# Weight copies in quarters instead of halves, and a second exponential buffer in the prefix pass

## The chip, the cores and the metric

One Trainium2 chip, all 8 cores, each running the same program on its own data with no exchange between them. Core c works on sequence c // 2 and on half c % 2 of its 4096 positions. The time is the device time of the slowest core in microseconds.

## The reference

A block with a state space part and a quantised feed-forward part, both fed with the same normalised input, on x of shape (4, 4096, 1024):

```python
xn = _layernorm(x, axis=-1)
x = x + _L0_attn_ref(xn, ...) + _L0_ffn_ref(xn, w_gate, w_up, w_down)

# _L0_attn_ref, D_MODEL 1024, D_INNER 2048, D_STATE 16:
x = _rmsnorm(resid, norm_w)
skip = x @ skip_w.T
x = x @ in_w.T
x = silu(_causal_depthwise_conv(x, conv_w, conv_b))
A = -jnp.exp(A_log)
delta = softplus(x @ wd1.T @ wd2.T + wd2_b)
Bm = x @ wb.T
Cm = x @ wc.T
# scan over positions: h = exp(dt*A) * h + (dt*x) * B ; y = sum_n h * C
y = _selective_scan(x, delta, Bm, Cm, A)
y = (y + x * W_D) * silu(skip)
return resid + y @ out_w.T
```

## The kernel before

A core owns 2048 positions (T) of a sequence. The state with which the scan of its half starts depends on the first half of the sequence, so every core also works through that prefix (`x_pre`), and a mask makes the result zero where the core owns the first half. D is 1024, E (the inner width) 2048 and thus 16 tiles of 128 channels (`ET`), the states are 16 (`NS`), taken 8 at a time (`nh`), and positions go in chunks of 512 (`CH`, 4 of them).

The stages in order of time: quantising and transposing of the feed-forward weights with the normalisation of the own half; the feed-forward part; the normalisation of the prefix; `p3_chunks` for the prefix; then `p3_prefix` and `p3_chunks` for the own half, interleaved by `drive`; `p3_scan` for the own half; the output projection.

`p3_chunks` first copies its weights into SBUF as bf16. `inwT` (1024 x 2048 float32) is taken as 8 blocks of 128 rows and each block in two halves: SyncE loads a half (128 x 1024 float32, 512 KB) into `tmpc`, and VectorE casts it into `inw_sb`. There is one `tmpc`, and SyncE waits for the last cast before the next load. For the own half `skipwT` follows in the same way, into `skw_sb`. Then come the four chunks; the first matmul of the first chunk waits for all of VectorE's work so far.

`p3_prefix` computes the state at the end of the prefix without a scan for each state: for each tile of 128 channels it loads delta (`dtile`) and x (`xct`), forms `dxt` (their product) and `cbuf` (the running sum of delta), and 8 biases. Then, for each of 8 states, ScalarE computes E = exp(scale * cbuf + bias) into `Eb[j]`, VectorE the product `ub` = dxt * B, and then the sum over positions of E * ub, in place in `Eb[j]` with its sum in `acc1`, which is copied to a column of `h0_sb`. `Eb` is `[xct, xct]`, so both entries are the tile that held x, and `E_free` is the count of VectorE's work after which ScalarE may write E again. Four small matmuls a step, whose results nobody uses, follow VectorE's instructions on TensorE.

`drive` gives one tile of `p3_prefix` and one chunk of `p3_chunks` alternately: tile 0, then the weight copies and chunk 0, tile 1, chunk 1, and so on; after chunk 3 the other 28 of 32 tiles stand alone. Each engine takes its instructions in the order written. Two helpers issue most of them: VectorE's all have line 54 and each waits for the one before it; ScalarE's have line 103; loads have line 130 and wait for the load before them on the same semaphore.

Of the kernel before, what the change touches and what calls it, by code (L numbers as in the profile page):

```python
# [14 lines left out]
D, E, NS, DTR, I, T = 1024, 2048, 16, 64, 2816, 2048  # L15
# [160 lines left out]
def build_nc(upto="full", dbg=None):  # L176
    nc = bass.Bass("TRN2", target_bir_lowering=False)
    kb = KB(nc)
# [6 lines left out]
    inwT = dr("inwT", [D, E])  # L185
    skipwT = dr("skipwT", [D, E])
# [343 lines left out]
    with contextlib.ExitStack() as st:  # L530
        sb = lambda n, s, dt=F32: st.enter_context(nc.sbuf_tensor(n, s, dt))
# [160 lines left out]
    def p3_chunks(xrT_src, own, sdel, sxcd, sBd, sCd, psums=None):  # L692
      def _gen():
        with contextlib.ExitStack() as st:
            sb = lambda n, s, dt=F32: st.enter_context(nc.sbuf_tensor(n, s, dt))
            pre = "c3o" if own else "c3p"
            inw_sb = sb(pre + "_inw", [128, 8, E], BF16)
            tmpc = sb(pre + "_tmpc", [128, E // 2])
            _xi0 = sb(pre + "_xi0", [128, 3 + CH])
            xib = [_xi0, _xi0]  # L700
            cb = sb(pre + "_cb", [128, CH])
# [7 lines left out]
            if own:  # L709
                skw_sb = sb(pre + "_skw", [128, 8, E], BF16)  # L710
# [8 lines left out]
            else:  # L719
                ps_x, ps_dl, ps_B, ps_C, ps_d2, ps_sk = psums  # L720

            for dt_ in range(8):
                for hh in range(2):
                    @B.sync
                    def _(sync):
                        kb.wait(sync, "V")
                        kb.wait(sync, "S")
                        kb.wait(sync, "St")
                        kb.wait(sync, "Tn")
                        kb.dma(sync, tmpc[:], inwT.rearrange("(a p) e -> p a e", p=128)[:, dt_, hh * (E // 2):(hh + 1) * (E // 2)])  # L730
                    ldv = kb.cnt["L"]

                    @B.vector
                    def _(vector):
                        vector = kb.wrap(vector, "V")
                        kb.wait(vector, "L", ldv)
                        kb.inc(vector.tensor_copy(inw_sb[:, dt_, hh * (E // 2):(hh + 1) * (E // 2)], tmpc[:]), "V")
            if own:
                for dt_ in range(8):
                    for hh in range(2):  # L740
                        @B.sync
                        def _(sync):
                            kb.wait(sync, "V")
                            kb.dma(sync, tmpc[:], skipwT.rearrange("(a p) e -> p a e", p=128)[:, dt_, hh * (E // 2):(hh + 1) * (E // 2)])
                        ldv = kb.cnt["L"]

                        @B.vector
                        def _(vector):
                            vector = kb.wrap(vector, "V")
                            kb.wait(vector, "L", ldv)  # L750
                            kb.inc(vector.tensor_copy(skw_sb[:, dt_, hh * (E // 2):(hh + 1) * (E // 2)], tmpc[:]), "V")

            for c in range(NCH):
                sba = SBatch(kb)
# [137 lines left out]
                sba.flush(B)  # L892
                yield
      return _gen()

    if upto == "p1pre":
# [197 lines left out]
    def p3_prefix():  # L1094
        with contextlib.ExitStack() as st:
            sb = lambda n, s, dt=F32: st.enter_context(nc.sbuf_tensor(n, s, dt))
            Brep = sb("pf_Brep", [128, 8, T], BF16)
            dtile = sb("pf_dt", [128, T])
            xct = sb("pf_xct", [128, T])
            dxt = sb("pf_dxt", [128, T])  # L1100
            Eb = [xct, xct]
            ub = sb("pf_ub", [128, T])
            cbuf = sb("pf_c", [128, T])
            onescol = sb("pf_ones", [128, 1])
            bias2 = sb("pf_bias", [128, NS])
# [5 lines left out]
            @B.vector  # L1111
            def _(vector):
                vector = kb.wrap(vector, "V")
                vector.memset(onescol[:], 1.0)
                vector.tensor_scalar(nA_sb[:], A_sb[:], -1.0, None, ALU.mult)

            E_free = [kb.cnt["V"], kb.cnt["V"]]

            for nh in range(2):
                @B.sync  # L1120
                def _(sync):
                    kb.wait(sync, "V")
                    kb.wait(sync, "S")
                    if nh == 0:
                        kb.wait(sync, "St")
                    kb.dma(sync, Brep[:], sB[nh * 8:nh * 8 + 8, :].partition_broadcast(128))
                ldb = kb.cnt["L"]

                for et in range(ET):
                    @B.sync  # L1130
                    def _(sync):
                        kb.wait(sync, "V")
                        kb.wait(sync, "S")
                        kb.dma(sync, dtile[:], sdelta[et * 128:(et + 1) * 128, :])
                        kb.dma(sync, xct[:], sxc[et * 128:(et + 1) * 128, :])
                    ldt = kb.cnt["L"]

                    @B.vector
                    def _(vector):
                        vector = kb.wrap(vector, "V")  # L1140
                        kb.wait(vector, "L", max(ldt, ldb))
                        vector.tensor_tensor(dxt[:], dtile[:], xct[:], ALU.mult)
                        vector.tensor_tensor_scan(cbuf[:], ones, dtile[:],
                                                  zero1[:], ALU.mult, ALU.add)
                    v_dx = kb.cnt["V"]

                    sba = SBatch(kb)
                    s_E = [0] * 8
                    v_bias = [0] * 8
                    for n in range(8):  # L1150
                        col = et * NS + nh * 8 + n

                        @B.vector
                        def _(vector):
                            vector = kb.wrap(vector, "V")
                            vector.tensor_tensor(bias2[:, n:n + 1], A_sb[:, col:col + 1],
                                                 cbuf[:, T - 1:T], ALU.mult)
                        v_bias[n] = kb.cnt["V"]

                    for n in range(8):  # L1160
                        j = n % 2
                        col = et * NS + nh * 8 + n
                        sba.wait("V", v_bias[n])
                        if E_free[j]:
                            sba.wait("V", E_free[j])
                        s_E[n] = sba.act(Eb[j][:], cbuf[:], AF.Exp,
                                         scale=nA_sb[:, col:col + 1],
                                         bias=bias2[:, n:n + 1])

                        @B.vector  # L1170
                        def _(vector):
                            vector = kb.wrap(vector, "V")
                            vector.tensor_tensor(ub[:], dxt[:], Brep[:, n, :], ALU.mult)
                            kb.wait(vector, "S", s_E[n])
                            vector.scalar_tensor_tensor(Eb[j][:], Eb[j][:], 1.0, ub[:],
                                                        ALU.mult, ALU.mult, accum_out=acc1[:])
                            E_free[0] = E_free[1] = kb.cnt["V"]
                            vector.tensor_copy(h0_sb[:, col:col + 1], acc1[:])
                        v_pf = kb.cnt["V"]

                        @B.tensor
                        def _(tensor):
                            for pc in (v_pf - 2, v_pf - 1, v_pf):
                                kb.wait(tensor, "V", pc)
                                tensor.matmul(ps_hp[:], eye_sb[:], eye_sb[:, 0:128],  # L1185
                                              start=True, stop=True)
                            kb.inc(tensor.matmul(ps_hp[:], eye_sb[:], eye_sb[:, 0:128],
                                                 start=True, stop=True), "Tn")
                    sba.flush(B)
                    yield  # L1190
# [23 lines left out]
    with contextlib.ExitStack() as st:  # L1214
        sb = lambda n, s, dt=F32: st.enter_context(nc.sbuf_tensor(n, s, dt))
        oww = sb("c4_oww", [128, ET, D], BF16)
        tmpc = sb("c4_tmp", [128, D])
# [130 lines left out]
```

How the kernel before makes its waits and increments, by code:

```python
        def wrapped(*a, **k):  # L51
            if kb.cnt[sem] > 0:
                eng.wait_ge(kb.sems[sem], kb.cnt[sem])
            instr = attr(*a, **k)
            instr.then_inc(kb.sems[sem], 1)
            kb.cnt[sem] += 1
            return instr
# [28 lines left out]
        @B.scalar  # L86
        def _(scalar):
            for it in items:
                if it[0] == "wait":
                    _, sem, v = it
                    scalar.wait_ge(kb.sems[sem], v)
                else:
                    _, my, out, in_, func, scale, bias, accum_out = it
                    if my > 1:
                        scalar.wait_ge(kb.sems["S"], my - 1)
                    kw = {}
                    if scale is not None:
                        kw["scale"] = scale
                    if bias is not None:
                        kw["bias"] = bias
                    if accum_out is not None:
                        kw["accum_out"] = accum_out
                    scalar.activation(out=out, in_=in_, func=func, **kw).then_inc(kb.sems["S"], 1)
# [23 lines left out]
    def dma(self, eng, out, in_, sem="L"):  # L127
        if self.cnt[sem] > 0:
            eng.wait_ge(self.sems[sem], self.cnt[sem])
        return self.inc(eng.dma_start(out=out, in_=in_), sem, 16)
# [1 line left out]
    def wait(self, eng, sem, val=None):  # L132
        v = self.cnt[sem] if val is None else val
        if v > 0:
            eng.wait_ge(self.sems[sem], v)
```

## Time and profile before

| | us |
|---|---|
| median of 2 runs | 11219.18 |
| lowest and highest | 11208.52, 11229.85 |
| profiled execution, its device time | 11207.93 |
| its span, slowest core | 11206.4 |
| spans of the eight cores | 11175.8 to 11206.4 |

The profile is that of the slowest core. The span is the time from its first instruction to its last, 1.5 us less than the execution's device time. The eight cores lie within 0.3% of each other, with a mean granted TensorE clock of 0.641 to 0.645 of full speed. The stage with `p3_prefix` in it runs from about 4998 to 8259 us.

### The profile page before, as it was taken

The numbers are of one execution on the slowest core, as the hardware profiler recorded it, in microseconds if no ns is written. First come the engines' busy times: TensorE is split into PE (matmuls) and PEld (weight loads), VectorE is DVE, ScalarE is ACT, GpSimd is POOL, SyncE is SP. The second block draws the span as 40 slices with busy tenths as digits, with TensorE's granted clock in tenths as the row PEclk, the third lists the DMA queues.
The fourth block names the chain that finished last, engine by engine and source line by source line (L and its number), as shares of the span: only waits on it lengthen the run. The fifth ranks groups of instructions, "written<-read, shape, count | busy, mean of one in ns | idle before, by whom it ended". The sixth has DMA issues, their size and how long they took to land.

```text
span 11206.4 us, 49419 instructions; the slowest of 8 cores (11175.8 to 11206.4 us)
## 1 busy us (share of the span) xinstructions
PE 2902.3 (26%) x8880; PEld 961.5 (9%) x8880; DVE 5942.8 (53%) x6033; ACT 2255.6 (20%) x2926; POOL 0.2 (0%) x4
## 2 busy tenths in 40 slices
PE   0101111454454123322344321111112222222224
PEld 0000000111111000000011100000000000000001
DVE  4444444344344122222323347777779997999950
ACT  1111111111111312210211222323322222222200
POOL 0000000000000000000000000000000000000000
PEclk9999999776676555555556555555555555555557
DMA  1111111100101011112111111010011112111112
GB/s 35 34 37 30 34 38 43 41 12 18 53 29 36 27 47 38 38 53 72 43 50 32 42 47 38 30 53 33 35 71 45 43 37 80 53 67 52 68 60 72
DMA packets 222951, 493.65 MB, mean 44 GB/s; under 512 B 115328, under 2 KB 115968, under 8 KB 198272
## 3 DMA queue, kind: packets, MB, share of 16 engines
q1 hardware_dynamic: 222656, 490.49, 13.0%
q8 instruction: 90, 1.47, 0.1%
q14 instruction: 205, 1.68, 0.1%
HBM read 330.27 MB, written 160.17 MB: 44 GB/s over the span
## 4 chain that ended last, share of the span: by engine, by line
DVE 52%; DMA 15%; PE 14%; ACT 9%; issue 9%; DVEq 1%; ACTq 1%; SPq 0%
DVE s3o_hb L54 10%; DVE pf_xct L54 5%; DVE pf_ub L54 5%; DVE s3o_ub L54 5%; DVE s3o_hcb L54 3%; PE c3o_pssk L834 2%; PE c3p_psx L768 2%; DVE c3o_cb L54 2%; DVE c3p_cb L54 2%; DVE q_t L54 2%; ACT L103 2%; DMA pf_dt<-sdelta 1%; DMA pf_xct<-sxc 1%; ACT q_wide L103 1%; PE c3o_psx L768 1%
## 5 line engine op out<-in xcount | busy, mean ns | idle before, releaser
L54 DVE TENSOR_TENSOR_SCAN s3o_hb<-s3o_ab,h_sb,s3o_ub 128x2048 bf16<-128x2048 f32 x256 | 1147.7, 4483 | 83.9 <-ACT s3o_ab L103 58.5
L103 ACT ACTIVATE s3o_ab<-s3o_dt,A_sb 128x2048 f32<-128x2048 f32 x256 | 513.1, 2004 | 1427.5 <-DVE s3o_hb L54 1412.8
L103 ACT ACT_TABLE_LOAD x196 | 251.5, 1283 | 2477.3 <-PE q_ps L389 845.9
L1031 PE MATMUL s3o_psht<-eye_sb 128*128 128x128 bf16 x768 | 203.3, 265 | 1859.8 <-DVE s3o_hb L54 1164.1
L103 ACT ACTIVATE pf_xct<-pf_c,pf_bias,pf_nA 128x2048 f32<-128x2048 f32 x256 | 536.8, 2097 | 676.2 <-DVE pf_xct L54 655.7
L1185 PE MATMUL pf_psht<-eye_sb 128*128 128x128 bf16 x768 | 201.5, 265 | 1756.3 <-DVE pf_ub L54 1207.0
L54 DVE TENSOR_TENSOR pf_ub<-pf_dxt,pf_Brep 128x2048 f32<-128x2048 f32 x256 | 586.9, 2293 | 27.3 <-DVE h_sb L54 0.8
L54 DVE SCALAR_TENSOR_TENSOR pf_xct<-pf_xct,pf_ub 128x2048 f32<-128x2048 f32 x256 | 586.8, 2292 | 27.4 <-DVE pf_ub L54 0.9
L54 DVE TENSOR_TENSOR s3o_ub<-s3o_dxt,s3o_Brep 128x2048 f32<-128x2048 f32 x256 | 586.8, 2292 | 27.0 <-DVE s3o_dxt L54 0.5
L1038 PE MATMUL s3o_psy<-s3o_hcb,eye_sb 128*128 128x512 bf16 x1024 | 477.4, 620 | 3.0 <-issue 0.6
L389 PE MATMUL q_ps<-eye_sb,q_wq 128*128 128x128 bf16 x528 | 140.2, 266 | 1212.7 <-DVE q_wq L54 868.1
L54 DVE TENSOR_TENSOR p_h<-p_h,p_psu 128x512 f32<-128x512 f32 (+1 forms) x96 | 61.8, 643 | 739.3 <-ACT p_h L103 739.3
L54 DVE TENSOR_REDUCE q_bm<-q_w 128x64 f32<-128x1024 f32 (+1 forms) x52 | 78.4, 1507 | 561.3 <-DMA q_w<-wu 202.0
L54 DVE TENSOR_TENSOR s3o_hcb<-s3o_hb,s3o_Crep 128x2048 bf16<-128x2048 bf16 x256 | 313.7, 1225 | 27.5 <-DVE s3o_hb L54 0.9
L103 ACT ACTIVATE p_hqT<-p_pst 128x128 bf16<-128x128 bf16 x352 | 97.9, 278 | 979.9 <-PE p_pst L623 979.9
L54 DVE COPY c3o_xi<-halo_sb 128x3 f32<-128x3 f32 x64 | 10.8, 169 | 532.3 <-ACT c3o_xi L103 532.3
L583 PE MATMUL p_psg<-p_wgh,xqT_sb 128*128 128x512 bf16 (+1 forms) x768 | 236.5, 469 | 170.5 <-DMA p_wdh<-swdT 75.3
L54 DVE TENSOR_TENSOR pf_dxt<-pf_dt,pf_xct 128x2048 f32<-128x2048 f32 x32 | 73.4, 2292 | 377.6 <-DMA pf_xct<-sxc 377.6
L1031 PEld LDWEIGHTS s3o_psht<-eye_sb 128*128 128x128 bf16 x768 | 79.8, 104 | 2166.1 <-issue 2166.1
L623 PE MATMUL p_pst<-eye_sb,p_hq 128*128 128x128 bf16 x352 | 87.9, 250 | 605.6 <-DVE p_hq L54 457.0
L1185 PEld LDWEIGHTS pf_psht<-eye_sb 128*128 128x128 bf16 x768 | 79.9, 104 | 1898.2 <-issue 1898.2
L638 PE MATMUL p_psd<-p_wdh,p_hqT 128*128 128x512 bf16 x352 | 217.2, 617 | 55.1 <-ACT p_hqT L103 55.1
(161 smaller groups left out, 5846.0 us busy)
## 6 DMA issues: line engine op xcount, KB each, us to landing
pf_dt<-sdelta SPq DMA_DIRECT2D x32, 1024.0 KB, 4.8
pf_xct<-sxc SPq DMA_DIRECT2D x32, 1024.0 KB, 4.8
s3o_dt<-sdelta_o SPq DMA_DIRECT2D x32, 1024.0 KB, 6.5
s3o_xct<-sxc_o SPq DMA_DIRECT2D x32, 1024.0 KB, 4.8
sxc<-c3p_xc SPq DMA_DIRECT2D x64, 256.0 KB, 2.3
sdelta<-c3p_db SPq DMA_DIRECT2D x64, 256.0 KB, 2.3
sxc_o<-c3o_xc SPq DMA_DIRECT2D x64, 256.0 KB, 2.3
sskip<-c3o_skb SPq DMA_DIRECT2D x64, 256.0 KB, 2.3
```

Source lines behind the costliest of these rows:

```text
L54: instr = attr(*a, **k)
L103: scalar.activation(out=out, in_=in_, func=func, **kw).then_inc(kb.sems["S"], 1)
L389: kb.inc(tensor.transpose(qps[pj][:], wqbf[j][:, jt * 128:(jt + 1) * 128], eye_sb[:]), "Tn")
L583: tensor.matmul(ps_g[jsi][:, :sl], xqT_sb[:, kd, tt * 128:(tt + 1) * 128], wgh[:, kd, s0:s0 + sl], start=(kd == 0), stop=(kd == 7))
L623: kb.inc(tensor.transpose(ps_t[pj][:], hq[jsp][:, isub * 128:(isub + 1) * 128], eye_sb[:]), "Tn")
L638: tensor.matmul(ps_d0[:], hqT[jsp][:, isub, :], wdh[:, it, 0:512], start=first, stop=last)
L768: mi = tensor.matmul(ps_x[jx][:], inw_sb[:, kd, et * 128:(et + 1) * 128], xrT_src[:, kd, c0:c0 + CH], start=(kd == 0), stop=(kd == 7))
L834: mi = tensor.matmul(ps_sk[:], skw_sb[:, kd, et * 128:(et + 1) * 128], xrT_src[:, kd, c0:c0 + CH], start=(kd == 0), stop=(kd == 7))
L1031: tensor.matmul(ps_ht[:], eye_sb[:], eye_sb[:, 0:128], start=True, stop=True)
L1038: mi = tensor.matmul(ps_y[sg][:], eye_sb[:], hcb[j][:, sg * 512:(sg + 1) * 512], start=(n == 0), stop=(n == 7))
L1185: tensor.matmul(ps_hp[:], eye_sb[:], eye_sb[:, 0:128], start=True, stop=True)
```

## The change

Three edits. The staging tile `tmpc` becomes half as wide (E // 4 columns), and the weight copies of `p3_chunks`, for the prefix and for the own half, take each block of 128 rows in four quarters instead of two halves. In `p3_prefix`, `Eb` gets a second buffer `_E1`, so that its two entries are different tiles, and `E_free` is kept for each of them. The tile for `ub` is dropped, and `ub` becomes another name of `dtile`.

```diff
-            tmpc = sb(pre + "_tmpc", [128, E // 2])
+            tmpc = sb(pre + "_tmpc", [128, E // 4])
...
+            EQ = E // 4
             for dt_ in range(8):
-                for hh in range(2):
+                for hh in range(4):
                     @B.sync
                     def _(sync):
                         kb.wait(sync, "V")
                         kb.wait(sync, "S")
                         kb.wait(sync, "St")
                         kb.wait(sync, "Tn")
-                        kb.dma(sync, tmpc[:], inwT.rearrange("(a p) e -> p a e", p=128)[:, dt_, hh * (E // 2):(hh + 1) * (E // 2)])
+                        kb.dma(sync, tmpc[:], inwT.rearrange("(a p) e -> p a e", p=128)[:, dt_, hh * EQ:(hh + 1) * EQ])
...
-                        kb.inc(vector.tensor_copy(inw_sb[:, dt_, hh * (E // 2):(hh + 1) * (E // 2)], tmpc[:]), "V")
+                        kb.inc(vector.tensor_copy(inw_sb[:, dt_, hh * EQ:(hh + 1) * EQ], tmpc[:]), "V")
             if own:
                 for dt_ in range(8):
-                    for hh in range(2):
+                    for hh in range(4):
                         @B.sync
                         def _(sync):
                             kb.wait(sync, "V")
-                            kb.dma(sync, tmpc[:], skipwT.rearrange("(a p) e -> p a e", p=128)[:, dt_, hh * (E // 2):(hh + 1) * (E // 2)])
+                            kb.dma(sync, tmpc[:], skipwT.rearrange("(a p) e -> p a e", p=128)[:, dt_, hh * EQ:(hh + 1) * EQ])
...
-                            kb.inc(vector.tensor_copy(skw_sb[:, dt_, hh * (E // 2):(hh + 1) * (E // 2)], tmpc[:]), "V")
+                            kb.inc(vector.tensor_copy(skw_sb[:, dt_, hh * EQ:(hh + 1) * EQ], tmpc[:]), "V")
...
-            Eb = [xct, xct]
-            ub = sb("pf_ub", [128, T])
+            _E1 = sb("pf_E1", [128, T])
+            Eb = [xct, _E1]
+            ub = dtile
...
-                            E_free[0] = E_free[1] = kb.cnt["V"]
+                            E_free[j] = kb.cnt["V"]
```

## Rows read from the trace of the kernel before

**Rows 1.** The page, part 1: busy us of each engine, share of the span, instructions.

```profile
PE 2902.3 (26%) x8880; PEld 961.5 (9%) x8880; DVE 5942.8 (53%) x6033; ACT 2255.6 (20%) x2926; POOL 0.2 (0%) x4
```

**Rows 2.** Busy time by stretch: the three weight copies (length, then each engine).

```profile
core 5: us, PE busy (x) PEld busy (x) DVE busy (x) ACT busy (x) POOL busy (x), PEclk, DMA share, GB/s
3950.60:4025.40 74.80, 0.00 (x1) 0.03 (x2) 11.11 (x16) 0.00 (x0) 0.00 (x0) 0.50 0.35 112
5074.50:5152.40 77.90, 0.01 (x1) 0.00 (x0) 11.11 (x16) 0.00 (x0) 0.00 (x0) 0.50 0.35 108
5152.40:5224.60 72.20, 0.00 (x0) 0.00 (x1) 11.11 (x16) 0.00 (x0) 0.00 (x0) 0.50 0.37 116
```

**Rows 3.** Timeline, start of the `skipwT` copy: start us, us, what, idle before.

```profile
5152.38 13.57 SPq L130 DMA_DIRECT2D c3o_tmpc<-skipwT  x4
5155.95 0.69 DVE L54 CAST c3o_skw<-c3o_tmpc 128x1024 bf16<-128x1024 f32 x1 [3.70 <-DMA c3o_tmpc<-skipwT]
5160.24 0.69 DVE L54 CAST c3o_skw<-c3o_tmpc 128x1024 bf16<-128x1024 f32 x1 [3.60 <-DMA c3o_tmpc<-skipwT]
```

**Rows 4.** Waits of the first matmuls for the last cast: own half, then prefix.

```profile
PE c3o_psx L768 <- DVE c3o_skw L54: 150.1, 1, 150.1
...
DVE c3p_inw L54: 75.5, 1
```

**Rows 5.** Timeline of the prefix loop, first two steps of a tile.

```profile
7619.92 1.28 ACT L103 ACT_TABLE_LOAD   x1 [20.52 <-DVE pf_bias L54]
...
7621.21 2.10 ACT L103 ACTIVATE pf_xct<-pf_c,pf_bias,pf_nA 128x2048 f32<-128x2048 f32 x1
7621.68 2.29 DVE L54 TENSOR_TENSOR pf_ub<-pf_dxt,pf_Brep 128x2048 f32<-128x2048 f32 x1
7624.08 2.29 DVE L54 SCALAR_TENSOR_TENSOR pf_xct<-pf_xct,pf_ub 128x2048 f32<-128x2048 f32 x1
...
7626.48 0.15 DVE L54 COPY h_sb<-pf_acc 128x1 f32<-128x1 f32 x1
...
7626.53 2.10 ACT L103 ACTIVATE pf_xct<-pf_c,pf_bias,pf_nA 128x2048 f32<-128x2048 f32 x1 [3.22 <-DVE pf_xct L54]
7626.74 2.29 DVE L54 TENSOR_TENSOR pf_ub<-pf_dxt,pf_Brep 128x2048 f32<-128x2048 f32 x1
...
7629.14 2.29 DVE L54 SCALAR_TENSOR_TENSOR pf_xct<-pf_xct,pf_ub 128x2048 f32<-128x2048 f32 x1
```

**Rows 6.** Groups of instructions, 4990 to 8260 us: the prefix loop's, with `dxt`.

```profile
L54 DVE TENSOR_TENSOR pf_ub<-pf_dxt,pf_Brep 128x2048 f32<-128x2048 f32 x256 | 586.9, 2293 | 27.3 <-DVE h_sb L54 0.8
L54 DVE SCALAR_TENSOR_TENSOR pf_xct<-pf_xct,pf_ub 128x2048 f32<-128x2048 f32 x256 | 586.8, 2292 | 27.4 <-DVE pf_ub L54 0.9
L103 ACT ACTIVATE pf_xct<-pf_c,pf_bias,pf_nA 128x2048 f32<-128x2048 f32 x256 | 536.8, 2097 | 676.2 <-DVE pf_xct L54 655.7 <-DVE h_sb L54 20.1
...
L54 DVE TENSOR_TENSOR pf_dxt<-pf_dt,pf_xct 128x2048 f32<-128x2048 f32 x32 | 73.4, 2292 | 377.6 <-DMA pf_xct<-sxc 377.6
```

**Rows 7.** Groups of VectorE with shapes apart: a cast of 128x512.

```profile
L54 DVE CAST c3o_xcbf<-c3o_xc 128x512 bf16<-128x512 f32 x64 | 27.3, 427 | 71.2 <-ACT c3o_xc L103 71.2
```

**Rows 8.** The staging tile of the own half: duration ns, starts, landing.

```profile
L130 SPq DMA_DIRECT2D c3o_tmpc<-inwT x16: 327/328/333, 5074.6 to 5147.6; - x16
L54 DVE CAST c3o_inw<-c3o_tmpc x16: 693/694/695, 5078.2 to 5151.6; 128x1024 bf16<-128x1024 f32 x16
...
DMA to landing us min/median/max: 3.3/3.5/4.4
```

**Rows 9.** DMA issues of the whole program: KB each, median us to landing.

```profile
pf_xct<-sxc SPq DMA_DIRECT2D x32, 1024.0 KB, 4.8
...
sxc<-c3p_xc SPq DMA_DIRECT2D x64, 256.0 KB, 2.3
...
c3p_tmpc<-inwT SPq DMA_DIRECT2D x16, 512.0 KB, 3.5
...
c3o_tmpc<-skipwT SPq DMA_DIRECT2D x16, 512.0 KB, 3.5
...
p_tmp<-wbT_c SPq DMA_DIRECT2D x1, 128.0 KB, 2.0
```

## Prediction

> **What bounds the kernel now.** I read the page's busy part first [rows 1]: VectorE is busy 53% of the span, ScalarE 20%, TensorE 26%. No engine fills the span, so what an edit is worth has to be read from its own stage. The diff touches two stages: the copying of weights at the start of `p3_chunks` (three times: `inwT` for the prefix, `inwT` and `skipwT` for the own half), and the inner loop of `p3_prefix`.
>
> The table by stage [rows 2] cuts out the three weight copies: 74.80, 77.90 and 72.20 us, together 224.9 us, in each of which VectorE is busy for 11.11 us (16 casts) and TensorE and ScalarE for nothing. That is a chain with no overlap: SyncE waits for the last cast, issues a load, VectorE waits for it, casts. The instructions in order of time [rows 3] show one round: the load is issued at 5152.38, the cast starts at 5155.95 (3.57 us later), lasts 0.69 us, and the next cast starts 4.29 us after this one. While this runs TensorE waits for the last cast: 150.1 us in the own half and 75.5 in the prefix [rows 4]. So the copies lie on the path in full.
>
> The prefix loop is the other case. In order of time [rows 5] its step is TENSOR_TENSOR (`ub`) 2.29 us, SCALAR_TENSOR_TENSOR with its sum 2.29, a column copy 0.15, and again: 5.06 us from one SCALAR_TENSOR_TENSOR to the next (7624.08 to 7629.14). The exponential of ScalarE, 2.10 us, starts at 7626.53, just after the sum is done with the one E buffer, runs beside the next `ub` product and ends at 7628.63. VectorE is done with `ub` at 7629.03 and starts the sum at 7629.14. So the exponential is ready 0.51 us before it is used. The groups of instructions say the same for all 256 steps [rows 6]: VectorE is idle for 27.4 us before the sums, 0.107 us each, and the same 27.3 before the `ub` products, which wait for nobody; its releaser is `pf_ub` on VectorE itself, not ScalarE. ScalarE does wait, 655.7 us in total, for the E buffer, but it is not the engine that is late.
>
> **The change, part by part.**
>
> *A second E buffer (`Eb = [xct, _E1]`, `E_free[j]`).* It takes away a wait of ScalarE: exponential n may start when sum n-2 is done instead of sum n-1. The chain through ScalarE is, per step, 0.16 us from the end of the sum to the exponential, 2.10 of exponential, about 0.11 to the sum and 2.29 of sum: 4.66 us, against VectorE's own chain of 5.06 [rows 5]. The longer one sets the pace and stays as it is: gain 0. From above the gain is bounded by all the idle time of VectorE before the sums, 27.4 us [rows 6]. At the first step of a tile the exponential starts late, since an activation table is loaded (1.28 us) after the biases are there; even there it ends at 7623.31 and is used at 7624.08, 0.77 us later [rows 5]. In the steady state exponential n starts at the end of sum n-2 and so again lies beside a `ub` product, one step ahead; only the second exponential of each tile moves to stand beside the first product and sum. VectorE's instructions should not lengthen by that: a product lasts 2293 ns with an exponential beside it (`ub`) and 2292 with ScalarE idle (`dxt`) [rows 6]. I cost this at 0.
>
> *`ub = dtile`.* The product goes into the tile that held delta. Both readers of delta, the `dxt` product and the scan, stand ahead of the first `ub` product on VectorE's own queue, and the next load of `dtile` already waits for everything of VectorE and ScalarE, before and after. No instruction and no wait is added: 0.
>
> *The weight copies in quarters.* 48 loads of 512 KB with 48 casts of 1024 columns become 96 loads of 256 KB with 96 casts of 512 columns; each round keeps its waits. Every wait, issue and landing is paid twice as often. The mean round is now 224.9 / 48 = 4.69 us. Of it two terms shrink. The cast: 128x1024 float32 to bf16 takes 694 ns [rows 8]; the very shape it becomes, 128x512, takes 427 [rows 7], so 0.27 less. The landing: 3.5 us for 512 KB [rows 8, 9]. A load of 256 KB is not in the trace. From below, 128 KB took 2.0; stores of 256 KB, to DRAM with the same 2 KB rows, took 2.3. From above, the step from 1024 KB (4.8) to 512 KB (3.5) is 1.3 us, and half of that off again gives 2.85; and at worst it doesn't shrink, 3.5 [rows 9]. Between the loads of 128 KB (2.0) and 512 KB (3.5) a straight line gives 2.5, and this is the value I take: it lies between the store and the extrapolation. So a round shrinks by 1.0 + 0.27 = 1.27 us:
>
> 2 x 224.9 - 96 x 1.27 = 449.8 - 121.9 = 327.9 us, which is 103 more than 224.9.
>
> The same with the ends: landing 2.0 gives +55, 2.3 gives +84, 2.85 gives +137, 3.5 gives +199. Nothing hides any of it, as TensorE, ScalarE and the rest of VectorE's queue stand behind the last cast.
>
> The Trainium skill (DMA: Bandwidth & Descriptors, Anatomy of one DMA) fits a transfer to 2.0 us fixed and bytes over 436 GB/s, measured on the other issuing path; the estimate from it is 3.2 for 512 KB and 2.6 for 256 KB, a drop of 0.60 where I take 1.0, and the sum would be +142. The trace's 3.5 for 512 KB lies 0.3 above that fit. The page also advises loads of 1 MiB and more, so it speaks against halving them.
>
> The first queue entries behind these waits are the chunk's first matmuls; they start later by the sum, and with them all that follows. The prefix's tiles 1 to 3 stand behind the chunks on every engine and move too. Sum: 11207.9 (the profiled execution, span 11206.4) + 0 + 0 + 103 = 11311. The median of the runs is 11219.2, 11.3 higher; on it the sum is 11322. I forecast 11315, between the two.
>
> **The rivals.**
>
> *The small loads are hidden or cost nothing (no change, 11208 to 11219).* This needs a second load in flight. Against it: the copy into the quarter tile waits as the one into the half tile did, there is still one `tmpc`, and TensorE waited 150.1 us for the last cast [rows 4].
>
> *The second E buffer was what was missing (faster).* If the sum on VectorE waited for ScalarE, double buffering would pay. For: ScalarE's 655.7 us of waiting, which looks like lost time. Against: the idle time before the sum is no longer than before the product [rows 6]. To be over 2% faster, 224 us, on top of the 103 of the copies, it must save 327 / 256 = 1.28 us a step; the time would be 10,984 to 10,995. It decides only where the exponential is longer than 2.10 + 0.51 us or VectorE's chain under 4.66.
>
> *A small load takes as long as a large one or longer (slower by over 2%).* Place: the same 96 rounds. If no term shrinks, +224.9, which is 11433 to 11444, 2.0% over. This decides from a landing of 3.77 us (then 0.27 of the cast is made up). For: rows of 2 KB are the shorter ones, and the eight cores load at once; single landings reach 4.4 us now [rows 8]. Against: each class of smaller load landed sooner [rows 9].
>
> *VectorE is slowed by ScalarE running ahead.* Were the sums a tenth longer, 256 x 0.23 = 59 us more: 11370 to 11381. It decides from any lengthening at all, since VectorE has no slack. No row shows a sum beside an exponential; against it stand the products, 2293 and 2292 ns, with and without one [rows 6].
>
> **How the numbers follow.** The forecast's case, the copies on the path with a landing between 2.0 and 3.5 and the prefix loop unmoved, has 0.88 and 11263 (11207.9 + 55) to 11418 (11219.2 + 199). Hidden loads 0.03, faster through the E buffer 0.02, no shrinking at all 0.04, slowed VectorE 0.03. I cut the upper end a little, since a landing of over 3.3 us contradicts three classes of rows: the range is 11260 to 11400, and the case of the slowed VectorE lies in it. Within 2%, about what a measurement of this kernel can tell from no change: 0.94. Slower by over 2% 0.04, faster 0.02.
>
> **What would show it.** In the profile after: 32 loads of 256 KB in each of the three copies, landing near 2.5 us; casts of 427 ns; the three copies 110, 113 and 105 us long, give or take 15; TensorE's wait for `skw` near 218 us instead of 150. In the prefix loop still 5.06 us per step, VectorE idle about 27 us before the sums, and ScalarE's wait for them down to about 192 x 2.96 = 570 us (two exponentials of each of 32 tiles now start without it). A step shorter than 5.06 would refute my reading of the loop; landings of 3.5 would refute the size of the copies' cost.

## The result

| | us |
|---|---|
| before, median of 6 runs | 11225.01 |
| after, median of 7 runs (11334.58 to 11347.67) | 11342.9 |
| ratio, 95% interval | 1.0109 (1.0097 to 1.0122) |
| profiled execution after, span of its slowest core | 11339.0 |

The change costs 1.1%, some 118 us between the medians and 132.6 us between the spans of the two profiled executions (11206.4 and 11339.0). The slowest core is core 7 now and was core 5. The page's first part after the change:

```profile
PE 2904.6 (26%) x8880; PEld 964.3 (9%) x8880; DVE 5951.1 (52%) x6081; ACT 2252.2 (20%) x2926; POOL 0.2 (0%) x4
```

Against [rows 1] no engine has more than 8.3 us of work added: VectorE has 48 more instructions (the casts) and 8.3 us more. So over 120 us came as waiting. The busy time by stretch, the three weight copies after the change (length, then each engine, as in [rows 2]), tells where:

```profile
3951.80:4071.20 119.40, 0.00 (x0) 0.00 (x0) 13.62 (x32) 0.00 (x0) 0.00 (x0) 0.50 0.23 70
5127.60:5245.70 118.10, 0.00 (x0) 0.00 (x0) 13.67 (x32) 0.00 (x0) 0.00 (x0) 0.50 0.23 71
5245.70:5360.80 115.10, 0.00 (x0) 0.00 (x0) 13.66 (x32) 0.00 (x0) 0.00 (x0) 0.50 0.25 73
```

They last 352.6 us together where they lasted 224.9: 127.7 of the 132.6 us. The staging tile of the own half, the first matmul's wait, and the loads' landing (the time from the issue of a load until its data is there), which answer to [rows 4, 8, 9]:

```profile
L54 DVE CAST c3o_inw<-c3o_tmpc x32: 426/427/428, 5130.5 to 5245.1; 128x512 bf16<-128x512 f32 x32
...
  PE c3o_psx L769: 233.4, 1
...
DMA to landing us min/median/max: 2.7/2.8/3.6
```

A cast takes 427 ns instead of 694, a load lands after 2.8 us instead of 3.5, and there are twice as many of both; TensorE waits 233.4 us for the last cast instead of 150.1.

The prefix loop, groups of instructions from 4990 to 8400 us, answers to [rows 6] (`ub` is shown as `pf_dt` now, since it shares delta's tile):

```profile
L54 DVE TENSOR_TENSOR pf_dt<-pf_dxt,pf_Brep 128x2048 f32<-128x2048 f32 x256 | 586.9, 2293 | 27.8 <-DVE h_sb L54 1.5
L54 DVE SCALAR_TENSOR_TENSOR pf_xct<-pf_xct,pf_dt 128x2048 f32<-128x2048 f32 x128 | 293.4, 2292 | 13.7 <-DVE pf_dt L54 0.5
L54 DVE SCALAR_TENSOR_TENSOR pf_E<-pf_E,pf_dt 128x2048 f32<-128x2048 f32 x128 | 293.4, 2292 | 14.0 <-DVE pf_dt L54 0.9
L103 ACT ACTIVATE pf_xct<-pf_c,pf_bias,pf_nA 128x2048 f32<-128x2048 f32 x128 | 267.9, 2093 | 224.8 <-DVE pf_xct L54 216.6 <-DVE h_sb L54 7.8
L103 ACT ACTIVATE pf_E<-pf_c,pf_bias,pf_nA 128x2048 f32<-128x2048 f32 x128 | 267.9, 2093 | 288.1 <-DVE pf_E L54 278.6 <-DVE h_sb L54 6.5
```

The two halves of the sums have 293.4 us each, the 586.8 of before; VectorE's idle time before them is 13.7 + 14.0 = 27.7 us (27.4 before). Only ScalarE's idle time changed, from 676.2 to 512.9 us. The timeline of one tile shows it running ahead:

```profile
7698.01 2.29 DVE L54 SCALAR_TENSOR_TENSOR pf_xct<-pf_xct,pf_dt 128x2048 f32<-128x2048 f32 x1
...
7700.46 2.09 ACT L103 ACTIVATE pf_xct<-pf_c,pf_bias,pf_nA 128x2048 f32<-128x2048 f32 x1 [1.04 <-DVE pf_xct L54]
7700.67 2.29 DVE L54 TENSOR_TENSOR pf_dt<-pf_dxt,pf_Brep 128x2048 f32<-128x2048 f32 x1
7703.07 2.29 DVE L54 SCALAR_TENSOR_TENSOR pf_E<-pf_E,pf_dt 128x2048 f32<-128x2048 f32 x1
...
7705.52 2.09 ACT L103 ACTIVATE pf_E<-pf_c,pf_bias,pf_nA 128x2048 f32<-128x2048 f32 x1 [2.96 <-DVE pf_E L54]
...
7708.12 2.29 DVE L54 SCALAR_TENSOR_TENSOR pf_xct<-pf_xct,pf_dt 128x2048 f32<-128x2048 f32 x1
```

The exponential into `pf_xct` at 7700.46 is ready at 7702.55 and is used at 7708.12, 5.57 us later, where it was 0.51 us in [rows 5]. And the sums still start 5.06 and 5.05 us apart.

### The profile page after: what moved, and what is told of

Read it like the earlier page. It is cut to its first block, busy times and chain, and to the rows that moved or that the text cites. A ratio compares the mean times of both kernels' runs of the same rounds, so it can differ in the third digit from the quotient of the medians.

```text
span 11339.0 us, 49803 instructions; the slowest of 8 cores (11322.2 to 11339.0 us)
## 1 busy us (share of the span) xinstructions
PE 2904.6 (26%) x8880; PEld 964.3 (9%) x8880; DVE 5951.1 (52%) x6081; ACT 2252.2 (20%) x2926; POOL 0.2 (0%) x4
## 4 chain that ended last, share of the span: by engine, by line
DVE 51%; DMA 16%; PE 13%; ACT 9%; issue 9%; DVEq 1%; ACTq 1%; SPq 0%
DVE s3o_hb L54 10%; DVE pf_dt L54 5%; DVE s3o_ub L54 5%; DVE s3o_hcb L54 3%; DVE pf_xct L54 3%; DVE pf_E L54 3%; PE c3o_pssk L835 2%; PE c3p_psx L769 2%; DVE c3p_cb L54 2%; DVE c3o_cb L54 2%; DVE q_t L54 2%; ACT L103 2%; DMA pf_dt<-sdelta 1%; DMA pf_xct<-sxc 1%; ACT q_wide L103 1%
## 5 line engine op out<-in xcount | busy, mean ns | idle before, releaser
L54 DVE TENSOR_TENSOR s3o_ub<-s3o_dxt,s3o_Brep 128x2048 f32<-128x2048 f32 x256 | 586.8, 2292 | 28.4 <-DVE s3o_hcb L54 2.3
L54 DVE TENSOR_TENSOR pf_dt<-pf_dxt,pf_Brep 128x2048 f32<-128x2048 f32 x256 | 586.9, 2293 | 27.8 <-DVE h_sb L54 1.5
L103 ACT ACTIVATE pf_E<-pf_c,pf_bias,pf_nA 128x2048 f32<-128x2048 f32 x128 | 267.9, 2093 | 288.1 <-DVE pf_E L54 278.6
L103 ACT ACTIVATE pf_xct<-pf_c,pf_bias,pf_nA 128x2048 f32<-128x2048 f32 x128 | 267.9, 2093 | 224.8 <-DVE pf_xct L54 216.6
L54 DVE SCALAR_TENSOR_TENSOR pf_E<-pf_E,pf_dt 128x2048 f32<-128x2048 f32 x128 | 293.4, 2292 | 14.0 <-DVE pf_dt L54 0.9
L54 DVE SCALAR_TENSOR_TENSOR pf_xct<-pf_xct,pf_dt 128x2048 f32<-128x2048 f32 x128 | 293.4, 2292 | 13.7 <-DVE pf_dt L54 0.5
```

The lines of the kernel that those rows point to most:

```text
L54: instr = attr(*a, **k)
L103: scalar.activation(out=out, in_=in_, func=func, **kw).then_inc(kb.sems["S"], 1)
```

## The experiments

The theory: the weight copies are a chain of latency in which every round counts in full, and the prefix loop is paced by VectorE, so that the second E buffer hides a wait nobody felt. The rivals: some of the 1.1% comes from the prefix edits, or hides a gain of theirs; or the second buffer does not do what it says. Every kernel below is the one before with only the edit named. Ratios are against runs of before on the same chip; the experiments ran on three chips, so kernels of different experiments are compared by their ratios.

### One part of the change at a time

Quarters only:

```diff
-            tmpc = sb(pre + "_tmpc", [128, E // 2])
+            tmpc = sb(pre + "_tmpc", [128, E // 4])
...
-                for hh in range(2):
+                for hh in range(4):
```

> The kernel before with the weight copies in quarters and nothing else. Theory (all of the cost is in the copies): the same three copies as in the changed kernel, some 352 us instead of 224.9, so +128 us of span and a ratio near 1.011. Rival (part of the 1% comes from the second E buffer or from ub = dtile): clearly less, under +100 us (1.009).

Measured: 11336.02 us against 11208.61, ratio 1.0111 (1.0095 to 1.0126).

The prefix edits only:

```diff
-            Eb = [xct, xct]
-            ub = sb("pf_ub", [128, T])
+            _E1 = sb("pf_E1", [128, T])
+            Eb = [xct, _E1]
+            ub = dtile
...
-                            E_free[0] = E_free[1] = kb.cnt["V"]
+                            E_free[j] = kb.cnt["V"]
```

> The kernel before with Eb = [xct, _E1], E_free[j] and ub = dtile, the copies left in halves. Theory (VectorE sets the pace of the loop): a step stays at 5.06 us, idle time before the sums stays at 27 us, ratio 0.999 to 1.001. Rival (the second buffer gives something that the copies hid): ratio 0.998 or less. Rival (ScalarE a step ahead slows VectorE): sums over 2.30 us and a ratio over 1.002.

Measured: 11211.44 against 11208.61, ratio 1.0001 (0.9992 to 1.0010). The sums of this kernel, groups of VectorE:

```profile
L54 DVE SCALAR_TENSOR_TENSOR pf_E<-pf_E,pf_dt 128x2048 f32<-128x2048 f32 x128 | 293.4, 2292 | 13.7 <-DVE pf_dt L54 0.5
L54 DVE SCALAR_TENSOR_TENSOR pf_xct<-pf_xct,pf_dt 128x2048 f32<-128x2048 f32 x128 | 293.4, 2292 | 13.7 <-DVE pf_dt L54 0.5
```

The two parts are 1.0111 and 1.0001, the whole 1.0109: within that 0.1% the cost is in the copies alone. A gain or loss of the prefix edits of over 0.1% is excluded.

### The size of a round

The same copies with one load of 1024 KB a block (`tmpc` of E columns, `range(1)`), and with eight of 128 KB (`E // 8`, `range(8)`):

> The kernel before with one load of 1024 KB and one cast of 2048 columns per block: 24 rounds instead of 48. Theory (a round costs a fixed part and a part by size): landing 4.8, cast 1.22, and 0.47 between them as now, 6.5 us a round, 156 us in all, -69 us against before, ratio 0.994. Rival (only the bytes count): 225 us as before, ratio 1.000.

> The kernel before with loads of 128 KB and casts of 256 columns: 192 rounds. Cast 0.29, between them 0.46. If the landing falls along the straight line of my prediction, to 2.0: 2.75 us a round, 528 us, +303 us, ratio 1.027. If it goes on falling as from 512 to 256 KB (by 2.6 ns per KB): 2.5, 3.25 us a round, 624 us, +399 us, ratio 1.036.

Measured: whole rows 11135.13, ratio 0.9932 (0.9918 to 0.9945); eighths 11565.37, ratio 1.0314 (1.0300 to 1.0328). The staging tile of each for the own half, whole rows first:

```profile
L130 SPq DMA_DIRECT2D c3o_tmpc<-inwT x8: 327/328/334, 5046.0 to 5093.9; - x8
L54 DVE CAST c3o_inw<-c3o_tmpc x8: 1226/1228/1228, 5051.8 to 5098.9; 128x2048 bf16<-128x2048 f32 x8
...
DMA to landing us min/median/max: 4.7/4.8/5.8
```

and eighths:

```profile
L130 SPq DMA_DIRECT2D c3o_tmpc<-inwT x64: 327/328/333, 5198.2 to 5392.9; - x64
L54 DVE CAST c3o_inw<-c3o_tmpc x64: 293/294/296, 5200.7 to 5395.4; 128x256 bf16<-128x256 f32 x64
...
DMA to landing us min/median/max: 2.3/2.3/3.0
```

A round of whole rows is 6.5 us (the copies of the three weights, from first issue to the end of the last cast, are 156.6 us in 24 rounds), as expected. A round of an eighth is 3.03 us (580.9 us in 192 rounds), between the two values I had put down, with a landing of 2.3 between 2.0 and 2.5. The landing by size is thus 4.8, 3.5, 2.8 and 2.3 us for 1024, 512, 256 and 128 KB: halving the load took off 1.3, 0.7 and 0.5 us, never half. The 2.3 is that of core 6. In the prefix's copy of the eighths the median is 2.3 on every core with an even number and 2.1 on every core with an odd one, while the quarters of the changed kernel take 2.9 and 2.8 there. So on the odd cores, core 7 among them, the last halving took off 0.7. The sum of the copies goes 156.6, 224.9, 352.6, 580.9 us.

### Does the second buffer take the wait away?

If the exponential had too little slack, the second buffer should matter. Each exponential is computed twice into the same tile, which doubles ScalarE's work and leaves the values as they are; once with one E buffer, once with the change's two (and its `ub = dtile`):

```diff
-                        s_E[n] = sba.act(Eb[j][:], cbuf[:], AF.Exp,
-                                         scale=nA_sb[:, col:col + 1],
-                                         bias=bias2[:, n:n + 1])
+                        for _rep in range(2):
+                            s_E[n] = sba.act(Eb[j][:], cbuf[:], AF.Exp,
+                                             scale=nA_sb[:, col:col + 1],
+                                             bias=bias2[:, n:n + 1])
```

> The kernel before with each exponential of the prefix loop computed twice into the same tile (ScalarE's work per step doubled, result unchanged), one E buffer. Theory (the exponential has 0.5 us of slack with one buffer, no more): the chain end of sum, two exponentials, sum becomes 0.16 + 2.10 + 0.2 + 2.10 + 0.11 + 2.29 = 7.0 us a step instead of 5.06, so +1.9 x 256 = +490 us less what the first steps hide, ratio 1.035 to 1.045. Rival (ScalarE is far off the path in this loop): ratio under 1.01.

> The same doubled exponentials with Eb = [xct, _E1], E_free[j] and ub = dtile. Theory (the second buffer does let ScalarE run a step ahead, it only had nothing to give): ScalarE needs 4.5 us a step, less than VectorE's 5.06, so the loop stays at 5.06 but for about 1.5 us at the start of each of 32 tiles, some +50 us, ratio 1.003 to 1.008. Rival (the second buffer does not take the wait away): as with one buffer, ratio 1.035 to 1.045.

Measured: one buffer 11690.84, ratio 1.0425 (1.0410 to 1.0441); two buffers 11272.09, ratio 1.0052 (1.0037 to 1.0066). Timeline with one buffer:

```profile
7902.90 2.29 DVE L54 SCALAR_TENSOR_TENSOR pf_xct<-pf_xct,pf_ub 128x2048 f32<-128x2048 f32 x1 [1.95 <-ACT pf_xct L103]
...
7905.35 4.28 ACT L103 ACTIVATE pf_xct<-pf_c,pf_bias,pf_nA 128x2048 f32<-128x2048 f32 x2 [2.62 <-DVE pf_xct L54]
7905.56 2.29 DVE L54 TENSOR_TENSOR pf_ub<-pf_dxt,pf_Brep 128x2048 f32<-128x2048 f32 x1
7909.80 2.29 DVE L54 SCALAR_TENSOR_TENSOR pf_xct<-pf_xct,pf_ub 128x2048 f32<-128x2048 f32 x1 [1.95 <-ACT pf_xct L103]
```

A step is 6.90 us (7.0 by the chain of the prediction), and VectorE's wait has ScalarE as its releaser, 1.95 us each time. The same with two buffers:

```profile
7703.92 2.29 DVE L54 SCALAR_TENSOR_TENSOR pf_E<-pf_E,pf_dt 128x2048 f32<-128x2048 f32 x1
...
7706.37 4.28 ACT L103 ACTIVATE pf_E<-pf_c,pf_bias,pf_nA 128x2048 f32<-128x2048 f32 x2 [0.78 <-DVE pf_E L54]
7706.58 2.29 DVE L54 TENSOR_TENSOR pf_dt<-pf_dxt,pf_Brep 128x2048 f32<-128x2048 f32 x1
7708.98 2.29 DVE L54 SCALAR_TENSOR_TENSOR pf_xct<-pf_xct,pf_dt 128x2048 f32<-128x2048 f32 x1
...
7739.64 2.29 DVE L54 SCALAR_TENSOR_TENSOR pf_xct<-pf_xct,pf_dt 128x2048 f32<-128x2048 f32 x1 [1.50 <-ACT pf_xct L103]
```

Here the two exponentials run until 7710.65 and thus beside most of the sum that starts at 7708.98, which still lasts 2.29 us: an exponential beside a sum doesn't slow it. The step is back at 5.06 us, and what is left is 1.50 us at the first sum of a tile, 32 x 1.5 = 48 us of the measured 54. With ScalarE's work doubled the same edit is worth 419 us; as the kernel is, nothing. So it works, and its worth hangs on whether the exponential is longer than the 2.10 + 0.51 us it may take.

### More than one load under way

Two staging tiles with a semaphore each; the next load is issued before this one is cast. The core of it:

```diff
-            tmpc = sb(pre + "_tmpc", [128, E // 2])
+            tmpcs = [sb(pre + f"_tmpc{j}", [128, E // 2]) for j in range(2)]
...
+            lds = [load(i) for i in range(2)]
+            for i in range(len(jobs)):
+                # wait for load i, cast tmpcs[i % 2], then:
+                if i + 2 < len(jobs):
+                    lds.append(load(i + 2))
```

> The kernel before with two staging tiles of 512 KB, each with a semaphore of its own, so that the next load is under way while this one is cast; 48 rounds as before. Theory (most of a round is latency, not transfer): two rounds of 4.69 us overlap, 2.35 us a round, 113 us instead of 224.9, -112 us, ratio 0.990. Rival (loads follow each other on the DMA engines and each keeps its full landing time): only the cast and the waits are hidden, 3.5 us a round, 168 us, -57 us, ratio 0.995.

The same with two tiles of E // 4, which is the change's piece in the memory of before:

> The kernel before with two staging tiles of 256 KB in the place of one of 512 KB, thus with the quarters of the change but two loads under way. Theory: two rounds of 3.67 us overlap, 1.84 us a round, 96 rounds, 176 us, -49 us against before, ratio 0.996. Rival (each load keeps its landing time of 2.9 for itself): 278 us, +53, ratio 1.005.

Measured: halves 11132.32, ratio 0.9919 (0.9903 to 0.9936); quarters 11190.19, ratio 0.9976 (0.9967 to 0.9986). DMA issues of the two, halves first:

```profile
c3o_tmpc<-inwT SPq DMA_DIRECT2D x16, 512.0 KB, 4.6
```

```profile
c3o_tmpc<-inwT SPq DMA_DIRECT2D x32, 256.0 KB, 3.0
```

In both the measured time lies between the theory and the rival. The halves' copies take 138.3 us in all, 2.88 us a round, where full overlap would be 2.35 and none 3.5: with two loads under way each lands after 4.6 us instead of 3.5. The quarters take 198 us, 2.06 a round (1.84 and 2.9 were expected), with a landing of 3.0 to 3.1. In both the saving of the copies (87 and 27 us) is the saving of the program (86 and 28 us). So against the kernel before, two quarter tiles under way save 28 us, where one alone cost 127, and two half tiles save 86, three times as much.

### The wait that VectorE does have in the prefix loop

In the groups of [rows 6] VectorE waits 377.6 us for `pf_xct`, the loads at the start of each tile. They can go early: delta's tile is free after the scan, and x's too if E has a tile of its own. The core of the edit (left out are the removal of the old loads, the first tile's loads ahead of the loop, two waits at its start, and the two aliases that make the room); for delta alone E stays in `xct`, and only `dtile` is loaded early:

```diff
-            Eb = [xct, xct]
+            _E1 = sb("pf_E1", [128, T])
+            Eb = [_E1, _E1]
...
                     v_dx = kb.cnt["V"]
+                    if (nh, et) != (1, ET - 1):
+                        en = (et + 1) % ET
+                        @B.sync
+                        def _(sync):
+                            kb.wait(sync, "V", v_dx)
+                            kb.dma(sync, dtile[:], sdelta[en * 128:(en + 1) * 128, :])
+                            kb.dma(sync, xct[:], sxc[en * 128:(en + 1) * 128, :])
```

> The kernel before, but the 8 KB of a further tile go to the wait that VectorE really has in the prefix loop: a single E tile of its own, so that xct is free after the dxt product and dtile after the scan, and both loads of the next tile are issued then, beside the eight steps (about 41 us) of this one. The room comes from two aliases (zb is cb, skb is db). Theory (VectorE's 377.6 us of waiting for pf_xct are on the path): about 10.1 us less in each of 30 tiles, -300 us, ratio 0.972 to 0.976; exponentials and sums as before, one E buffer being enough. Rival (the wait moves elsewhere, to other loads or into slower steps): 0.985 or more.

> The kernel before with only the load of delta taken early (its tile is free after the scan, no memory is needed); xct is loaded after the eighth step as before. Theory: one of two serial landings of 4.8 us goes, about 5 us in each of 31 tiles, -150 us, ratio 0.986 to 0.988. Rival: none of it shows, ratio 1.000.

Measured: both early 10889.4, ratio 0.9706 (0.9691 to 0.9720); delta alone 11062.87, ratio 0.9862 (0.9848 to 0.9877). The `dxt` group of each, both early first:

```profile
L54 DVE TENSOR_TENSOR pf_dxt<-pf_dt,pf_xct 128x2048 f32<-128x2048 f32 x32 | 73.4, 2293 | 40.0 <-DMA pf_xct<-sxc 22.6 <-DMA pf_Brep<-sB 14.2
```

```profile
L54 DVE TENSOR_TENSOR pf_dxt<-pf_dt,pf_xct 128x2048 f32<-128x2048 f32 x32 | 73.4, 2292 | 228.2 <-DMA pf_xct<-sxc 228.2
```

The idle time goes from 377.6 to 40.0 and 228.2 us, 338 and 149 less; the program is 330 and 156 us faster. With both early that is more than the 300 and the ratio of 0.972 to 0.976 that I had put down: I had left two tiles out, and they gain too, though the very first load and the reload of B are still waited for. With one E buffer of its own, ScalarE idles 676.4 us before its exponentials, as in the kernel before, and it costs nothing.

Both ideas in one kernel, with four staging tiles for the prefix and two quarters for the own half:

> Both together: the loads of the prefix pass taken early, and the weight copies with more than one load under way (prefix: four tiles of 512 KB; own half: two of 256 KB, which is all that fits). Theory: -300 from the prefix pass, -18 from the copies of the own half as measured with two quarters, -45 from the prefix's copy (75 to about 30), together -363 us, ratio 0.967 to 0.970. Rival (four loads under way are no faster than two, 2.9 us a round): -347, ratio 0.969 to 0.972.

Measured: 10812.6, ratio 0.9643 (0.9627 to 0.9659), the fastest of all, and by the two ratios (0.9643 and 1.0109) some 4.6% under the changed kernel. That is 407 us less than before where I had put down 363, and below the range of 0.967 to 0.970: 30 us of the difference are the early loads, as above. The prefix's staging tile:

```profile
L130 SPq DMA_DIRECT2D c3p_tmpc<-inwT x16: 327/328/328, 3953.0 to 3977.5; - x16
L54 DVE CAST c3p_inw<-c3p_tmpc x16: 693/694/694, 3958.4 to 3984.3; 128x1024 bf16<-128x1024 f32 x16
...
DMA to landing us min/median/max: 4.6/6.0/7.2
```

Its copy takes 32.0 us, 2.0 a round, though each load takes 6.0 us to land. The three copies are 168 us, 58 less than in the kernel with the early loads alone (226), while the program is 77 us faster than that one. In the profiled executions the slowest cores (4 and 0) differ by 81.8 us; of the 24 outside the copies 11 lie ahead of the first copy, where the two kernels are the same, 7 between the prefix's copy and the own half's, and 5 behind the last. Cores of a single execution differ by as much (with the early loads alone the first copy starts between 3928.7 and 3964.3 us), so no cause in the edit is shown for that rest.

## Why the prediction was right, point by point

- **The copies lie on the path in full.** Right: 127.7 us of added copies, 132.6 of added span, and 1.0111 with the quarters alone. The other 5 us add up from stretches that the change does not touch: 1.2 more before the first copy, 7.3 more between the prefix's copy and the own half's, 3.6 less behind the last. They compare core 7 of one execution with core 5 of another; between the medians the whole change is 118 us, and such differences have no cause shown here.
- **The cast.** 427 ns as taken from [rows 7]. Right to the nanosecond.
- **The landing of a 256 KB load, taken as 2.5 us.** This term was mis-sized: it measured 2.8 in the changed kernel (2.9 to 3.0 with the quarters alone). The step that failed is the straight line between 128 KB and 512 KB in [rows 9]. Its lower end was one load of a contiguous array (`wbT_c`, 2.0 us), while the weight loads take pieces out of rows of 8 KB. But that explains the smaller part. The eighths are 128 KB loads of the right kind, and they land after 2.1 us on the odd cores and 2.3 on the even ones: a line from there to the 3.5 to 3.6 of the halves would have given some 2.6 and 2.7, where 2.8 and 2.9 were measured. Most of the miss on core 7 is thus that the landing doesn't lie on a straight line between these sizes. The extrapolation from 1024 and 512 KB had said 2.85, and I had used it only as a bound. With 2.8 the prediction's sum is 449.8 - 96 x 0.97 = 357 us, +132, against 103 as written and 127.7 in the traces.
- **The forecast of 11315 was low by 28 us.** Half of that is the step above: the medians rose by 118 where 103 was written. The other 13 are the starting point, as the kernel before had a median of 11225.0 beside the change and I had added to about 11212.
- The Trainium skill (DMA: Bandwidth & Descriptors, Anatomy of one DMA) gives, by its fit, an estimate of 2.6 us for 256 KB and a drop of 0.6 from 512 KB; the trace has 2.8 and a drop of 0.7. The sum by it, +142, was 14 us above the 127.7, and my 103 was 25 below. The Trainium skill (DMA: Bandwidth & Descriptors, Bandwidth) also advises loads of 1 MiB and more. The trace agrees: the whole rows had the ratio 0.9932.
- **The second E buffer at 0.** Right: steps of 5.06 us and 1.0001 for the edit alone. The chain I had worked out for ScalarE (4.66 us a step) was checked from the other side, by doubling the exponential: 7.0 worked out, 6.90 measured.
- **ScalarE's waits down to about 570 us.** Measured 512.9 in the groups. I had overlooked that the third exponential of each tile also waits less, 1.04 us instead of 2.96, as it is one step late: 32 x 1.92 = 61 us. The mechanism stands; the size was short by that term.
- **`ub = dtile` at 0.** It was not run apart from the second buffer; the two together gave 1.0001.
- **The signs.** The copies were to be 110, 113 and 105 us, give or take 15, and are 119.4, 118.1 and 115.1; TensorE's wait was to be 218 us and is 233.4. All are long for the same reason.
- **The rivals.** Hidden loads: no, nearly every microsecond of the copies is in the span. A gain of the second buffer: no. A slower VectorE: no, 2292 ns a sum as before, and 2.29 us with an exponential beside it in the doubled kernel. No shrinking at all: no; it would have taken a landing of 3.77 us.

## What to carry to other kernels

A wait belongs on the account only of the engine that is late. ScalarE's 656 us of waiting for its buffer were worth nothing, as the data was ready 0.51 us before VectorE wanted it, while VectorE's own 378 us of waiting for loads in the same loop were worth 330: look at what the busiest engine of the stage waits for, and spend the memory there. In a chain of load, wait, cast with one staging tile the number of rounds sets the time, since halving a load takes off much less than half of its landing; make the pieces larger or keep two under way. And for the price of a load not in the trace, take two rows of the same kind and keep the result as a range: a straight line drawn down to a much smaller load came out 0.3 us too low here, and the step between the two larger sizes, halved, came close (2.85 for a measured 2.8 to 3.0).

## What the runs showed of the hardware that I had not expected

- The landing of a load fell faster toward the small sizes: from the medians, which are rounded to 0.1 us, I estimate 2.5 ns per KB from 1024 to 512 KB, about 3 from 512 to 256 and about 5 from 256 to 128.
- The same 128 KB load landed after 2.3 us on the even cores and 2.1 on the odd ones (prefix's copy in eighths). Single loads of 128 KB of contiguous arrays took 1.8 to 2.3 over all runs, most of them 2.0, so a difference by layout alone is not shown.
- Loads under way together delay each other before the DMA engines are full: 512 KB lands after 3.5 us alone, 4.6 with one other and 6.0 with three others, while the time per load falls from 4.69 (with its cast) to 2.88 and 2.0 us. The DMA engines' busy share in the prefix's copy was 0.35, 0.58 and 0.82.
